# A decoder's routing stage: ScalarE normalises the second token tile of each batch, VectorE the first

## What is computed

```python
def _layernorm(x, axis=-1, eps=1e-05):
    m = jnp.mean(x, axis=axis, keepdims=True)
    v = jnp.var(x, axis=axis, keepdims=True)
    return (x - m) / jnp.sqrt(v + eps)

# x = _layernorm(x); 16 batches, 32 experts, 8 tokens chosen by each expert
logits = jnp.einsum('bsd,ed->bse', x, gate_w) + gate_b
probs = jax.nn.softmax(logits, axis=-2)                  # over the 256 tokens
vals_t, idx_t = jax.lax.top_k(probs.transpose(0, 2, 1), 8)
tok = jnp.take_along_axis(x, flat_idx[:, :, None], axis=1)
merged = jnp.einsum('bked,bke->bed', tok, vals)          # one row for each batch and expert
h = gelu(concat(merged, 1) @ w1); o = concat(h, 1) @ w2  # each expert's two layers
```

## Time and profile before

| | us |
|---|---|
| median of 3 runs | 3905.18 (3896.85 to 3906.78) |
| the profiled execution's own time | 3899.97 |
| its span, first to last instruction | 3898.2 |
| routing stage within the span | about 1932.3 to 2017.7 |
| experts after it | about 2019.3 to 2640 |

### The profile page before, as it was taken

How to read it: one execution, slowest core, us unless ns; L and a number is a source line. 1 busy time by engine, 2 the same in 40 slices (tenths; PEclk the granted TensorE clock), 3 DMA queues, 4 the chain that set the end, 5 groups by cost and what they waited for, 6 DMA issues and landing times. The chain is left out here.

```text
span 3898.2 us, 70083 instructions
## 1 busy us (share of the span) xinstructions
PE 3375.3 (87%) x22932; PEld 2351.4 (60%) x22940; DVE 1961.9 (50%) x4906; ACT 1271.1 (33%) x4328; POOL 1414.1 (36%) x2092
## 2 busy tenths in 40 slices
PE   4999999999997999999767566667999699999945
PEld 3777677677674788888531111114777588888821
DVE  5555455455453565666440000004665476676657
ACT  2222223223222555555320000001111466666621
POOL 2555455455452343434210000001222255555537
PEclk9999999999999999999877877778999899999976
DMA  5000000000001111111279999992111211111123
GB/s 129 23 16 16 32 16 16 32 16 16 32 11 68 40 57 49 59 48 59 79 297 428 427 427 429 427 406 88 65 68 55 91 44 43 65 43 55 42 71 132
DMA packets 140018, 440.28 MB, mean 113 GB/s; under 512 B 37840, under 2 KB 41296, under 8 KB 119440
## 3 DMA queue, kind: packets, MB, share of 16 engines
q1 hardware_dynamic: 135856, 435.23, 29.0%
q10 hardware_dynamic: 4096, 4.20, 0.3%
HBM read 392.74 MB, written 46.66 MB: 113 GB/s over the span
## 5 line engine op out<-in xcount | busy, mean ns | idle before, releaser
L431 POOL TENSOR_TENSOR cross_prob<-cross_prob,cross_rsum 128x256 f32<-128x256 f32 (+1 forms) x1024 | 548.5, 565 | 721.6 <-DVE cross_rsum L816 717.5
L678 ACT ACTIVATE cross_prob<-cross_S,cross_neg_max 128x256 f32<-128x256 f32 (+1 forms) x1024 | 445.4, 459 | 53.1 <-DVE cross_neg_max L811 46.0
L431 POOL TENSOR_TENSOR self_prob<-self_prob,self_rsum 128x128 f32<-128x128 f32 (+1 forms) x512 | 246.8, 507 | 193.3 <-DVE self_rsum L816 189.2
L590 PE MATMUL cross_T<-cross_ident,cross_prob 128*128 128x128 f32 x1792 | 290.0, 279 | 11.0 <-DVE cross_probT L821 7.7
L1210 PE MATMUL experts_H<-moe_w,experts_tok 128*32 128x512 f32 x1024 | 167.5, 814 | 130.2 <-DMA moe_b<-in_L_ffn_w 123.4
L590 PEld LDWEIGHTS cross_T<-cross_ident,cross_prob 128*128 128x128 f32 x1792 | 205.6, 142 | 70.9 <-issue 38.4
L821 DVE COPY cross_probT<-cross_T 128x384 f32<-128x384 f32 (+1 forms) x256 | 158.9, 621 | 166.0 <-PE cross_T L590 165.9
L678 ACT ACTIVATE self_prob<-self_S,self_neg_max 128x128 f32<-128x128 f32 (+1 forms) x512 | 209.5, 424 | 82.5 <-DVE self_neg_max L809 82.5
L1350 POOL MEMSET norm_minus_half<- 128x2 f32 x1 | 0.1, 105 | 626.0 <-POOLq L53 626.0
L534 PE MATMUL self_A<-self_wo_f,self_zT 128*128 128x512 f32 x512 | 225.1, 593 | 0.6 <-DVE self_zT L828 0.6
L678 ACT ACTIVATION_READ_ACCUMULATOR cross_prob<-cross_S,cross_neg_max 128x1 f32 x1024 | 223.0, 218 | 0.0
(11 more groups left out here) (273 smaller groups left out, 8813.7 us busy)
## 6 DMA issues: line engine op xcount, KB each, us to landing
moe_w<-in_L_ffn_w SPq DMA_DIRECT2D x64, 4096.0 KB, 34.8
cross_x_t<-x SPq DMA_DIRECT2D x32, 512.0 KB, 5.2
cross_c_t<-in_ctx SPq DMA_DIRECT2D x32, 512.0 KB, 6.0
cross_res<-x SPq DMA_DIRECT2D x32, 512.0 KB, 3.6
x<-cross_res SPq DMA_DIRECT2D x32, 512.0 KB, 2.8
self_x_t<-in_x SPq DMA_DIRECT2D x16, 512.0 KB, 4.7
self_res<-in_x SPq DMA_DIRECT2D x16, 512.0 KB, 3.6
x<-self_res SPq DMA_DIRECT2D x16, 512.0 KB, 2.8
```

What stands on the lines that cost most here:

```text
L431: ins = pool.tensor_tensor(pr, pr, rsum[:, h, t:t + 1].to_broadcast([P, KQ[t]]), ALU.mult)
L590: mm = pe.transpose(TP[:, o:o + P], prob[:, h % NP, SOFF[t] + k * P:SOFF[t] + (k + 1) * P], ident[:, :])
L678: ins = act.activation(prob[:, h % NP, SOFF[t]:SOFF[t] + KQ[t]], SC[h % 4][:, SOFF[t]:SOFF[t] + KQ[t]], ACT.Exp, bias=neg_max[:, h, t:t + ...
```

## The change

The second tile's `apply` goes from VectorE to ScalarE, as an ACTIVATE with the function Identity, scale = rstd and bias = shift, both one value for each partition. VectorE computes shift = -mean times rstd with one instruction of 128x1 (`scalar_tensor_tensor`), ahead of its own tile. `stats_of(n)` gets a wait for ScalarE's tile of batch n-2, whose mean and rstd slot it overwrites. TensorE waits for both tiles. In ScalarE's program `apply_second(n + 1)` stands ahead of `taken(n)`, and behind `exps(g)`.

```diff
             rstd = r.sb("rstd", [P, 2, T])
+            shift = r.sb("shift", [P, 2])
...
                 def stats_of(n):
                     dve.wait_ge(x_ok[n], 16)
+                    if n >= 2:
+                        dve.wait_ge(normed_1, n - 1)
...
                 def apply(n):
                     dve.wait_ge(ln_pow, n + 1)
+
+                    dve.scalar_tensor_tensor(shift[:, n % 2:n % 2 + 1], mv[:, n % 2, 1, 0:1], -1.0, rstd[:, n % 2, 1:2], ALU.mult, ALU.mult).then_inc(shifts, 1)
                     x = x_of(n)
-                    for t in range(T):
-                        ins = dve.tensor_scalar(x[:, t, :], x[:, t, :], mv[:, n % 2, t, 0:1], rstd[:, n % 2, t:t + 1], ALU.subtract, ALU.mult)
-                    ins.then_inc(normed, 1)
+                    dve.tensor_scalar(x[:, 0, :], x[:, 0, :], mv[:, n % 2, 0, 0:1], rstd[:, n % 2, 0:1], ALU.subtract, ALU.mult).then_inc(normed_0, 1)
...
+                def apply_second(n):
+                    act.wait_ge(shifts, n + 1)
+                    x = x_of(n)
+                    act.activation(x[:, 1, :], x[:, 1, :], ACT.Identity, bias=shift[:, n % 2:n % 2 + 1], scale=rstd[:, n % 2, 1:2]).then_inc(normed_1, 1)
...
+                apply_second(0)
                 for n in range(n_batch):
                     g = n // G - 1
                     if g >= 0 and n % G == 1:
                         exps(g)
+                    if n + 1 < n_batch:
+                        apply_second(n + 1)
                     taken(n)
...
                 def transposes(n):
-                    pe.wait_ge(normed, n + 1)
+                    pe.wait_ge(normed_0, n + 1)
+                    pe.wait_ge(normed_1, n + 1)
```

More of the change, by code:

```diff
@@ L949, in expert_phase @@
             x_ok = [r.sem(f"x_ok{n}") for n in range(n_batch)]
-            ln, ln_pow, pool_const, normed = (r.sem(n) for n in ("ln", "ln_pow", "pool_const", "normed"))
+            ln, ln_pow, pool_const, shifts, normed_0, normed_1 = (r.sem(n) for n in "ln ln_pow pool_const shifts normed_0 normed_1".split())
             g_full, g_ok, t_full, t_ok, l_full, l_ok, mx, ex, step, sel_full, sel_ok, m_full, m_ok, mt_full, mt_ok, stored = (
```

## The result

| | before | after |
|---|---|---|
| median of 8 runs | 3900.21 us (3896.85 to 3906.78) | 3911.97 us (3904.91 to 3914.01) |
| ratio to before | | 1.0028, 95% interval 1.0019 to 1.0037 |
| own time of the profiled execution | 3899.97 | 3910.8 |
| its span | 3898.2 | 3909.0 |
| routing stage, first bn_stats to the experts' first token copy | 82.97 | 92.94 |

The account below looks back on a forecast made before the run. No engine fills the routing stage, so the order of work decides. Group terms sum to 13A - 1.99 = +8.2 us; from a start of 3902.6 this gives 3910.8, rounded to 3911, range 3903 to 3919.

Parts of the forecast that it names:

- The start: Time of the kernel before, put at 3902.6 us, between the profiled execution's own time and the median of three runs.
- the sum: Routing stage's delays over all groups, 13A - 1.99, +8.2 us; against the profiled execution's own time it gives 3908.1.
- signs of being wrong: First new wait missing, merge or logits over 2 us where they took 1.9, or experts taking up the delay.
- 0.39 us a batch: VectorE's saving from one tile less, minus the shift instruction; 6.2 us over 16 batches if nothing waited.
- hidden anyway: Rival: VectorE's 3 to 4 us waits for logits absorb choose's delays; time about +1.5 us or below; chance 0.05.
- side by side: Rival: VectorE's and ScalarE's tiles overlap without a wait that bites; time 6 us below before; chance 0.03.
- No table load: Contradicts a rival: Identity and Exp not sharing a table, up to eight loads, +10.3 us; chance 0.01.
- A: Duration of ScalarE's 128x512 Identity on the second tile, taken as 0.78 us, bounds 0.60 and 0.81.
- 5A - 2.41: First group, up to logits(0): four new stats waits, then tile and copies ahead of logits; +1.49 us.
- 3A - 0.07: Each of two middle groups: delay of choose, one stats wait and later transposes; 2.27 us.
- 2A + 0.56: Last group: delay of choose and later transposes, without a stats wait between the two applies; 2.12 us.
- The clock, the term set at nothing: Rival: 2.4 GHz level comes later, each group losing up to 3.4 us; chance 0.16 in at least one group.

Follow-up runs that it names:

- e2: Kernel after, with four slots for mean, variance, rstd and shift, so stats_of waits for ScalarE's tile four batches back; stage 87.00 us, ratio 1.0014.
- e1: Kernel after, with the exponentials one iteration earlier in ScalarE's program, ahead of the tile; stage 86.44 us, ratio 1.0008.
- e3: Kernel after, but VectorE normalises both tiles, ScalarE only waits for the shift, and stats_of has no new wait; stage 86.24 us, ratio 1.0014.
- e5: Kernel after, with ScalarE's second tile behind the copies of taken(n) instead of ahead; stage 94.94 us, one execution alone.
- e6: Kernel after, with earlier exponentials and four slots together; stage 82.56 us, ratio to before 0.9996.
- e8: Kernel after, with TensorE's idle stretches filled by unused transposes of the identity; stage 90.41 us, ratio to before 1.0018.
- e9: Kernel before, with TensorE's idle stretches filled by unused transposes of the identity; stage 77.21 us, ratio 0.9990.

## Why the prediction came out as it did

**The time, and the luck in it.** 3911 was forecast and the median is 3911.97, but two misses cancel in this. The start, put at 3902.6, was 2.4 us above the median of the kernel before, 3900.21. The change, put at 8.2 us, is 11.8 between the medians and 10.8 between the profiled executions (3910.8 against the 3908.1 of the sum). The interval of 7 to 14 us contains 8.2. The stage was to be 8 us longer and is 9.97 longer, mostly by the clock's 1.6 us; the experts were to take as long as before and took 1.8 us more in the profiled execution. And one of the prediction's own signs of being wrong came true: two merges that had taken 1.9 us took 2.83 and 2.89.

**Foreseen rightly.** That VectorE wouldn't gain its 0.39 us a batch, since `stats_of` waits for the tile just released: 0.49 to 0.50 us of idle time each, forecast about 0.4 (e2 takes it away and gets the 2.21 us period). That choose would wait some 1.9 us three times for exponentials queued behind the tile and the copies: 1.88 (e1 takes it away). That the delay passes through TensorE's chain to the end of the stage and isn't absorbed: the rival "hidden anyway" falls with the four pieces, as does "side by side". No table load stands in the stage's timeline of ScalarE, as the earlier trace rows had let expect.

**The size of A.** ScalarE's instruction:

```profile
L1073 ACT ACTIVATE moe_w<-moe_w,route_shift,route_rstd x16: 807/813/817, 1938.8 to 2006.7; 128x512 f32<-128x512 f32 x16
```

It takes 0.813 us, the upper bound of 0.81 and not the 0.78 taken: this is the 0.632 of the Square, which reads SBUF, and 0.09 for each of the two pointer operands. The estimate by the Trainium skill's "ScalarE: Activation LUTs", section "What ACT_TABLE_LOAD costs", was 0.80, 0.01 below this row. With the measured value the sum 13A - 1.99 is 8.58, and the four pieces measured 8.53. By term, with A at 0.81 in each: first group 5A - 2.41 = 1.64 (measured 1.70), a middle group 3A - 0.07 = 2.36 (2.36 and 2.35), the last 2A + 0.56 = 2.18 (2.12).

**The strict order of the queue.** Copies and exponentials that were ready did stand behind a waiting instruction; e3 shows it with the wait alone, ahead of nothing. So far the traces agree with what the Trainium skill says of ScalarE, that it works off its queue strictly in order, in "TensorE: Matmul & The Clock Gate", section "Architectural detail: the array is 16× 32×32, not 1× 128×128".

**The clock, the term set at nothing.** The prediction put the merge 4.5 us after the start of transposes(6), thought this would do for the 2.4 GHz level as 4.3 had, and gave the contrary a chance of 0.16. It was the contrary in two of three groups, each at a third of the full price of 3.4 us. Windows of the kernel before, from transposes(6) on (the figure behind the busy times is the granted clock):

```profile
1964.35:1968.40 4.05, 3.86 (x17) 3.46 (x18) 3.90 (x14) 1.72 (x4) 0.95 (x2) 0.50 0.89 382
1968.40:1972.40 4.00, 4.00 (x52) 1.70 (x51) 1.07 (x4) 1.54 (x3) 0.92 (x1) 0.99 0.99 414
```

And of the kernel after:

```profile
1965.64:1970.30 4.66, 4.24 (x19) 3.54 (x19) 3.91 (x16) 2.93 (x6) 1.53 (x2) 0.50 1.01 415
1970.30:1972.20 1.90, 1.90 (x13) 0.59 (x16) 0.00 (x0) 1.26 (x3) 0.44 (x1) 0.51 1.03 431
1972.20:1975.00 2.80, 2.80 (x45) 1.19 (x35) 0.07 (x1) 0.60 (x1) 0.00 (x0) 1.00 0.97 403
```

Before, 4.05 us at 0.50 (1.2 GHz), with TensorE busy for 3.86 of them, and then 2.4 GHz from ahead of the merge on. After, the level rose 6.6 us after transposes(6) started, 1.9 into the merge: merge and last transposes cost 1.04 and 1.05 us more in two groups. In the third it rose 3.3 us after (the granted clock is 0.69 from 2009.60 to 2009.80, 0.50 ahead of it and 1.00 behind), and they cost 0.40 less. With 0.1 less for logits(0) that is the +1.6 of the table. So the step that failed is the argument that the rise would come as before because "the work in the stretch is the same and nearly as dense". The gap ahead of transposes(7) was 0.42 us in place of 0.19, and e5, with the same gap at 1.00, lost 3.64 - 1.92 = 1.72 us in all three merges. But the gap can't be all of it. In e2 and e6 there is none at this place, and yet merge(0) and merge(1) took 2.03 and 2.77 us in e2, 2.89 and 2.48 in e6. TensorE's timeline of e2, transposes(10), choice(1), transposes(11), merge(1):

```profile
1983.99 1.94 PE L1124 MATMUL route_X<-moe_ident,moe_w 128*128 128x128 f32 x8 [5.01 <-ACT route_xT L1068]
1985.72 0.64 PE L1143 MATMUL route_T<-moe_ident,route_pr 128*128 128x128 f32 x2
1986.19 1.94 PE L1124 MATMUL route_X<-moe_ident,moe_w 128*128 128x128 f32 x8
1988.07 2.77 PE L1152 MATMUL route_M<-moe_w,route_selT 128*32 128x512 f32 x16
```

TensorE was busy for all of the 4.08 us ahead of this merge, at a granted clock of 0.50. e8 gained in one group and lost in two. A stretch of TensorE's work as dense as before, or denser, is thus no ground for expecting the rise at the same point; what decides in a given group stays open.

## What to carry to other kernels

Moving work to an idle engine also moves a wait into that engine's order: all that is ready behind it now waits for the engine that you meant to relieve. Before such a move, look at what the new instruction stands ahead of (here exponentials that another engine comes to fetch) and whether the released buffer's reader is the very instruction just started; each needs its own repair, an earlier place and more slots, and both together gave back 9.4 us where the change had cost 8.5. Sum the pieces that the clock left alone apart from those that it can stretch: the first repeated to 0.01 us and in the kernel after followed the arithmetic to 0.1 each, the second moved by up to 2.0 us a group between kernels (e5 against before).

## What the runs showed of the hardware that was not expected

- The same merge, sixteen matmuls, took anything from 1.92 to 3.64 us, by where in it the granted clock rose; in two pairs of executions of one program each merge repeated to 0.1 us, and logits(0) to 0.2 (3.55 and 3.38 in the kernel after).
- 82 filler transposes, of no use to the result, made the stage of the kernel before 5.8 us shorter (82.97 to 77.21): 2.5 us up to the end of logits(0), 2.3 behind the last logits, 0.9 in the groups. In the kernel after, 94 of them gave 2.5 us. In the profiled execution of e9 the experts took 625.1 us, 620.4 and 620.7 in the two of before, so part of it may be given back later; the time's ratio of 0.9990 is 3.9 us. One execution doesn't settle that.
- In the thirteen profiled executions the routing stage began between 1930.9 and 1939.3 us, though the phases ahead of it are the same in all kernels: a scatter nearly as large as the effect. Without the cut into pieces of one stage no experiment here could have been read.
